# A bias that a rank-one matmul added, added by VectorE from a precomputed matrix

## The chip, the cores and the metric

The kernel runs on one core of a Trainium2 chip. The metric is the device time of the whole program in microseconds (us), lower is better. Engines are named as the profile names them: PE is TensorE's matmul, PEld its weight load, DVE is VectorE, ACT is ScalarE, POOL is GpSimd, SP is SyncE, which issues the DMAs.

## The reference, cut to what matters

The input is x of 8 batches x 1024 nodes x 128 features, and adj, a 1024 x 1024 matrix. Two blocks follow one another, each with a residual and a layer norm. The first is three graph layers whose weighting is adj squared element by element. The second is two graph layers with a bias, and then LSTMs over windows of 1, 2, 3 and 4 nodes; the last state of each window takes the place of its last node.

```python
h = relu(einsum('ts,bsh->bth', adj, x @ Wg0 + bg0))
h = relu(einsum('ts,bsh->bth', adj, h @ Wg1 + bg1))   # bg1 is the bias of this case
for p in range(1, 5):
    nw = T // p
    last = lstm_last(Wih[p-1], Whh[p-1], bih[p-1], bhh[p-1], h[:, :nw*p].reshape(B*nw, p, H))
    h = h.at[:, arange(nw)*p + (p-1)].set(last.reshape(B, nw, H))
```

Since adj @ (h @ Wg1 + bg1) = (adj @ h) @ Wg1 + rowsum(adj) x bg1, the bias of the second graph layer is an outer product: row sums of adj (one per node) times bg1 (one per feature). It is the same for every batch.

## The kernel before

**Numbers.** Every fp32 product is made of three matmuls on values that are split in a high and a low part (HI, LO): `product` at lines 514 to 518 issues them as L516, L517 and L518. So each result in PSUM is read twice: ACT writes HI with an activation (`hi_part`), then DVE writes LO as the difference (`lo_part` L966, or `lo_relu` L969 where a relu is in between).

**Stages.** The first block takes the batches in pairs (lines 530 to 647). The second block is a software pipeline of nine slots, 0 to 8. In slot n the graph layers of batch n are computed, and LSTM steps of the batches before it are put between them, so that PE has matmuls while ACT and DVE work. Slots 3 to 6 are a loop of two turns of two slots; the others are written out. The lists `SLOT`, `DRAIN` (slot 7) and `LAST` (slot 8), lines 256 to 279, set one order of items, and each engine goes through the same list in order, doing its own share of each item. No engine passes over an item that it waits for.

**Items that matter here.**
- `adj_x`, `wg0`, `adj_h`, `wg1` are the graph layers of a batch, each in two halves of 512 columns. `wg1` is the last: three matmuls of `product` on z (adj @ h) and the weights `wgs[:, i, 1, :]`, and then `bias_product`, L652, which adds brow x rowsum as one more matmul of 512 columns. ACT then writes h0 HI with a relu (L897, called at L950) and DVE h0 LO (L969, called at L1299).
- `wg0` has its bias already the other way: a matrix bias0 is made once in slot 0 (item `bias`, lines 762 to 768 and 936 to 939), DVE adds it to PSUM in place (L1288), ACT waits for that and writes HI (L943), DVE writes LO (L969).
- a step X, Y or Z with a window p and a step s is an LSTM step of a stream. PE makes its gates (3 for s = 0, else 4), ACT applies sigmoid or tanh to each (L911), DVE does the cell (L1208, or L1210, L1212, L1215), ACT the tanh (L921), DVE multiplies (L1229) and splits the state in HI and LO (L1246, L966) for the next step's matmuls. The tile is gates_x and hstep_x for X, gates and hstep for Y.
- `ahead` lets PE make the gates that don't depend on the state before it. The gates rotate through six PSUM banks: PE makes gate n only when ACT has acted on gate n - 6 (`gate_bank_free`, lines 696 to 700, checked before a step's first and third gate).
- `split` splits the next batch's x (ACT L818, DVE L966), `scale` is the layer norm's last part (L1024), `fin` puts the LSTM result back into xb (PE L805, DVE L1305).

**Order around the change** in slots 3 to 6: `adj_h` half 1, `split`, `wg1` half 0, step X 4 3, step Y 2 0, `wg1` half 1, `scale`, `fin` 0, step Y 2 1, `fin` 1. The cell of X 4 3 is finished together with Y 2 0. Slots 0 to 2 leave out what has no batch yet; in slot 1 the scaling of the last pair of the first block (`pair_scale`, L1024 x16) stands between Y 2 0 and `wg1` half 1. The first item of the next slot, Y 1 0, reads h0, so PE waits there for both halves.

Of the kernel before, what the change touches and what calls it, by code (L numbers as in the profile page):

```python
# [8 lines left out]
F32 = mybir.dt.float32  # L9
# [5 lines left out]
P = 128  # L15
# [24 lines left out]
def build(nc, x, adj_t, w1, w2, w3, wg0, bg0, wg1, bg1, wih_t, whh_t, bih, bhh, out):  # L40
# [10 lines left out]
    with ctx:  # L51
# [4 lines left out]
        def place(nbytes):  # L56
            at = top[0]
            top[0] += (nbytes + 63) // 64 * 64
            return at

        def sb(name, shape, dt, at=None):
            size = 4 * int(np.prod(shape[1:]))
            return nc.alloc_sbuf_tensor_at(name, shape, dt, offset=place(size) if at is None else at)
# [14 lines left out]
        adj_raw = sb("adj_raw", [P, MT, N], F32, big_at)  # L78
        lw = sb("lw", [P, 2, 2 * SKIPS - 1, G4], F32R, big_at)
        rowsum = sb("rowsum", [P, N], F32R, big_at + 28 * KB)  # L80
        r2_at = place(16 * KB)
        y2 = sb("y2", [P, 2, K2, N], F32R, r2_at)
        w0_raw = sb("w0_raw", [P, H1 + K2 * H2 + K3 * F], F32, r2_at)
# [66 lines left out]
        def sem(name):  # L150
            return ctx.enter_context(nc.semaphore(name))
# [21 lines left out]
        sum_mm, sum_hi, sum_lo = sem("sum_mm"), sem("sum_hi"), sem("sum_lo")  # L173
        bias_mm, bias_set = sem("bias_mm"), sem("bias_set")
        bias_add = sem("bias_add")
        lw_hi, lw_lo = sem("lw_hi"), sem("lw_lo")
        gate_mm = sem("gate_mm")
        gate_act = sem("gate_act")
# [334 lines left out]
        def _(pe):  # L513
# [136 lines left out]
            def bias_product(dst, stat, mov, start):  # L650

                return pe.matmul(dst, stat, mov, start=start, stop=True)  # L652

            def pe_slot(slot, turn):
# [18 lines left out]
                def mm_unit(r):  # L673
                    return ps[:, GB + r % 2, :]
# [8 lines left out]
                for item in items(slot):  # L683
# [43 lines left out]
                    elif item[0] == "adj_x":  # L727
                        _, half, m0, m1 = item
                        if m0 == 0:
                            bank_free(half)  # L730

                        def tile_split(m):
                            pe.wait_ge(b_lo, m + 1)
                        last = adj_by(mm_unit(half), lambda i, m: node[:, i, m * P:(m + 1) * P], half, m0, m1,
                                      tile_split if slot == 0 and half == 0 else None)
                        if m1 == MT:
                            last.then_inc(b_mm, 1)
                    elif item[0] == "wg0":

                        v = item[1]  # L740
                        bank_free(2 + v)
                        lo_reached(b_lo_of(slot, v))
                        for t in range(4):
                            nt = (4 * v + t) * P
                            dst = mm_unit(2 + v)[:, t * F:(t + 1) * F]
                            last = product(dst, lambda i: z[:, i, nt:nt + P], lambda i: wgs[:, i, 0, :],
                                           True, True)
                        last.then_inc(b_mm, 1)
                    elif item[0] == "rowsum":


                        pe.wait_ge(acc_lo, 1)
                        pe.wait_ge(const_set, 1)
                        for half in range(HALVES):
                            cols = slice(half * BANK, (half + 1) * BANK)
                            parts = [adj[:, i, m, cols] for m in range(ADDED, MT) for i in (HI, LO)]
                            parts += [h0[:, HI, cols], h0[:, LO, cols]]
                            for n, part in enumerate(parts):
                                last = pe.matmul(ps[:, half, :], ones[:], part, start=(n == 0),
                                                 stop=(n == len(parts) - 1))  # L760
                        last.then_inc(sum_mm, 1)
                    elif item[0] == "bias":

                        pe.wait_ge(sum_lo, 1)
                        for t in range(MT):
                            last = bias_product(ps[:, t // 4, t % 4 * F:(t % 4 + 1) * F],
                                                rowsum[:, t * P:(t + 1) * P], brow[:, 0, :], True)
                        last.then_inc(bias_mm, 1)
                    elif item[0] == "adj_h":
                        _, half, m0, m1 = item  # L770
                        if m0 == 0:
                            bank_free(4 + half)

                        def h_tile_ready(m):
                            lo_reached(b_lo_of(slot, 2 + m // 4))
                        last = adj_by(mm_unit(4 + half), lambda i, m: node[:, i, m * P:(m + 1) * P], half,
                                      m0, m1, h_tile_ready)
                        if m1 == MT:
                            last.then_inc(b_mm, 1)
                    elif item[0] == "wg1":  # L780

                        half = item[1]
                        bank_free(6 + half)
                        lo_reached(b_lo_of(slot, 4 + half))
                        cols = slice(half * BANK, (half + 1) * BANK)
                        product(mm_unit(half), lambda i: wgs[:, i, 1, :], lambda i: z[:, i, cols],
                                True, False)
                        bias_product(mm_unit(half), brow[:, 1, :], rowsum[:, cols], False).then_inc(b_mm, 1)
                    elif item[0] == "fin":

                        _, v, back = item
                        if v == 0:

                            last_step = before(slot, k, lambda w, b: b + w.back == back and w.p == SKIPS
                                               and w.s == SKIPS - 1)
                            pe.wait_ge(h_done, ahead("unit", slot, turn, k - last_step + 1))
                        if slot < B:
                            lo_reached(b_lo_of(slot, 6 + v))
                        else:

                            lo_reached(0)
                            pe.wait_ge(fin_add, ahead("fin", slot, turn, n_fin - 1))
                        for t in range(4):
                            at = (2 * v + t // 2) * OPEN_BLOCK + t % 2 * P
                            last = pe.transpose(mm_unit(v)[:, t * F:(t + 1) * F], full_in(slot, back)[:, at:at + P],  # L805
                                                ident_f[:])
                        last.then_inc(fin_mm, 1)
                        n_fin += 1
# [5 lines left out]
        def _(act):  # L814
# [78 lines left out]
            def act_slot(slot, turn):  # L893
                def hi_part(r, dst, func):

                    act.wait_ge(b_mm, ahead("mm", slot, turn, r + 1))
                    nc.scalar.activation(dst, ps[:, GB + r % 2, :], func).then_inc(b_hi, 1)  # L897

                k, gate, begun, n_ended = 0, 0, [], 0
                for item in items(slot):  # L900
# [29 lines left out]
                    if item[0] == "adj_x" and item[3] == MT:  # L930
                        hi_part(item[1], z[:, HI, cols], ACT.Copy)
                    elif item[0] == "rowsum":
                        act.wait_ge(sum_mm, 1)
                        nc.scalar.activation(h0[:, HI, :], ps[:, 0:2, :].rearrange("p a c -> p (a c)"),
                                             ACT.Copy).then_inc(sum_hi, 1)
                    elif item[0] == "bias":
                        act.wait_ge(bias_mm, 1)
                        for v in range(2):
                            nc.scalar.activation(bias0[v][:], ps[:, v, :], ACT.Copy).then_inc(bias_set, 1)
                    elif item[0] == "wg0":  # L940

                        act.wait_ge(bias_add, ahead("bias", slot, turn, item[1] + 1))
                        nc.scalar.activation(node[:, HI, cols], ps[:, GB + item[1], :], ACT.Relu).then_inc(b_hi, 1)  # L943
                    elif item[0] == "adj_h" and item[3] == MT:
                        hi_part(4 + item[1], z[:, HI, cols], ACT.Copy)
                    elif item[0] == "split":

                        x_hi(batch_of(slot, turn, -1), b_hi)
                    elif item[0] == "wg1":
                        hi_part(6 + item[1], h0[:, HI, cols], ACT.Relu)  # L950

            slots(act, act_slot)

# [8 lines left out]
        def _(dve):  # L962
# [220 lines left out]
            def dve_slot(slot, turn):  # L1183
# [12 lines left out]
                for item in items(slot):  # L1196
# [97 lines left out]
                    elif item[0] == "split":  # L1294
                        hi_ready(7)
                        x_lo(batch_of(slot, turn, -1), b_lo)
                    elif item[0] == "wg1":
                        hi_ready(7 + splits(slot) + item[1])
                        lo_relu(h0[:, LO, cols], ps[:, GB + item[1], :], h0[:, HI, cols], b_lo)  # L1299
                    elif item[0] == "fin":  # L1300
# [69 lines left out]
```

## Time and profile before

| | us |
|---|---|
| three runs, median (lowest to highest) | 1044.88 (1043.42 to 1046.79) |
| the profiled execution | 1043.99 |
| its span, first to last instruction | 1042.1 |
| TensorE's granted clock over the span, share of full speed | 0.991 |

The page gives each engine's busy time; the table of windows gives it for stretches of the span. The timeline has one line per instruction, or per run of equal ones: start, duration, engine, line, output and input, and in square brackets how long the engine had been idle and who released it. Durations of neighbours on one engine overlap, because they are pipelined, so what an instruction costs its engine is the distance from its start to the next start.

### The profile page before, as it was taken

What the parts mean: (1) busy time and instruction counts of PE and PEld (TensorE: products, weight loads), DVE (VectorE), ACT (ScalarE), POOL (GpSimd) and SP (SyncE); (2) the same over time, 40 slices, a digit from 0 to 9 for tenths busy, and PEclk for the clock granted to TensorE, in tenths of its full rate; (3) what the DMA queues carried; (4) which work ended last, traced back from release to release, by engine and by line L of the source; (5) the groups of instructions that cost most, each with busy time, mean ns of one, the idle gap of its engine ahead of it and who ended that gap; (6) DMA issues with size and microseconds to landing.
All of it is one profiled execution on the core that took longest, in us unless ns stands there. A gap on an engine that the chain in (4) does not pass through costs nothing.

```text
span 1042.1 us, 15018 instructions
## 1 busy us (share of the span) xinstructions
PE 1001.4 (96%) x5624; PEld 881.9 (85%) x5624; DVE 584.9 (56%) x1415; ACT 379.2 (36%) x696; POOL 19.8 (2%) x22
## 2 busy tenths in 40 slices
PE   5999999999999999999998999999999999999883
PEld 4888998889988899888987879898988989889782
DVE  7242533424334243342475576668677786777887
ACT  6221202212023120131334354546464454546652
POOL 0000000000000000000000000101010010100000
PEclk9999999999999999999999999999999999999997
DMA  9400000000000000000120000000000000000001
GB/s 315 124 1 1 1 1 1 1 1 2 1 0 0 0 0 0 0 0 0 56 105 1 1 1 1 1 1 1 21 1 21 0 20 0 21 1 21 1 15 46
DMA packets 21743, 20.42 MB, mean 20 GB/s; under 512 B 960, under 2 KB 18496, under 8 KB 21696
## 3 DMA queue, kind: packets, MB, share of 16 engines
q1 hardware_dynamic: 21696, 19.81, 6.0%
q8 instruction: 27, 0.44, 0.2%
q14 instruction: 20, 0.16, 0.1%
HBM read 15.61 MB, written 4.19 MB: 19 GB/s over the span
## 4 chain that ended last, share of the span: by engine, by line
PE 88%; DVE 8%; ACT 2%; issue 1%; DMA 0%; ACTq 0%; SPq 0%; DVEq 0%
PE ps L516 25%; PE ps L517 24%; PE ps L518 24%; PE ps L636 9%; PE ps L615 4%; PE ps L618 1%; DVE adj L966 1%; DVE xb L1024 1%; ACT gates_last L911 1%; PE ps L805 0%; DMA xb<-in_x 0%; DVE gates_last L1229 0%; DVE node L966 0%; PE ps L652 0%; DVE square L1032 0%
## 5 line engine op out<-in xcount | busy, mean ns | idle before, releaser
L516 PE MATMUL ps<-adj,node 128*128 128x512 f32 x384 | 151.6, 395 | 12.7 <-DVE adj L966 10.0
L517 PE MATMUL ps<-adj,node 128*128 128x512 f32 x384 | 150.5, 392 | 0.0
L518 PE MATMUL ps<-adj,node 128*128 128x512 f32 x384 | 150.4, 392 | 0.0
L966 DVE TENSOR_TENSOR y<-ps,y 128x512 fp32r<-128x512 f32 x48 | 33.1, 691 | 186.0 <-ACT y L851 186.0
L851 ACT ACTIVATE y<-ps 128x512 fp32r<-128x512 f32 x48 | 28.7, 598 | 294.5 <-PE ps L518 294.4
L516 PE MATMUL ps<-adj,h 128*128 128x512 f32 x256 | 99.7, 389 | 0.0
L517 PE MATMUL ps<-adj,h 128*128 128x512 f32 x256 | 99.7, 389 | 0.0
L518 PE MATMUL ps<-adj,h 128*128 128x512 f32 x256 | 99.6, 389 | 0.0
L516 PEld LDWEIGHTS ps<-adj,node 128*128 128x128 f32 x384 | 72.6, 189 | 28.0 <-DVE adj L966 10.7
L969 DVE SCALAR_TENSOR_TENSOR h<-ps,h 128x512 fp32r<-128x512 f32 x112 | 76.5, 689 | 35.2 <-ACT h L851 34.4
L636 PE MATMUL ps<-s,adj 128*128 128x256 f32 x768 | 93.0, 283 | 0.0
L636 PEld LDWEIGHTS ps<-s,adj 128*128 128x128 f32 x768 | 92.4, 192 | 0.0
L911 ACT ACTIVATE gates<-ps,lb 128x512 f32<-128x512 f32 (+2 forms) x117 | 70.7, 649 | 43.4 <-PE ps L518 29.3
L518 PEld LDWEIGHTS ps<-adj,node 128*128 128x128 f32 x384 | 72.5, 189 | 15.5
L517 PEld LDWEIGHTS ps<-adj,node 128*128 128x128 f32 x384 | 72.7, 189 | 14.0
L911 ACT ACTIVATE gates_x<-ps,lb 128x258 f32<-128x258 f32 (+1 forms) x156 | 67.2, 508 | 34.4 <-PE ps L518 34.4
L851 ACT ACTIVATE h<-ps 128x512 fp32r<-128x512 f32 x96 | 57.4, 597 | 48.9 <-PE ps L518 46.0
L615 PE MATMUL ps<-w3s,h 128*128 128x256 f32 x256 | 59.6, 333 | 0.0
L618 PE MATMUL ps<-w3s,h 128*128 128x128 f32 x256 | 56.9, 222 | 0.0
L518 PEld LDWEIGHTS ps<-adj,h 128*128 128x128 f32 x256 | 48.1, 188 | 10.1
L516 PEld LDWEIGHTS ps<-adj,h 128*128 128x128 f32 x256 | 48.1, 188 | 9.8
L517 PEld LDWEIGHTS ps<-adj,h 128*128 128x128 f32 x256 | 48.1, 188 | 9.7
(213 smaller groups left out, 2028.7 us busy)
## 6 DMA issues: line engine op xcount, KB each, us to landing
square<-in_adj_t SPq DMA_DIRECT2D x8, 512.0 KB, 8.1
xb<-in_x SPq DMA_DIRECT2D x8, 512.0 KB, 7.5
adj_raw<-in_adj_t SPq DMA_DIRECT2D x8, 512.0 KB, 8.4
out<-xb SPq DMA_DIRECT2D x7, 512.0 KB, 3.2
lw_raw<-in_wih_t SPq DMA_DIRECT2D x1, 1024.0 KB, 5.7
lw_raw<-in_whh_t SPq DMA_DIRECT2D x1, 768.0 KB, 7.2
w_raw<-in_w SPq DMA_DIRECT2D x1, 512.0 KB, 11.0
out<-xb SPq DMA_DIRECT2D x2, 256.0 KB, 2.5
```

The lines of the kernel that those rows point to most:

```text
L516: pe.matmul(dst, stat(HI), mov(HI), start=start, stop=False)
L517: pe.matmul(dst, stat(HI), mov(LO), start=False, stop=False)
L518: return pe.matmul(dst, stat(LO), mov(HI), start=False, stop=stop)
L615: pe.matmul(ps[:, q % BANKS, 2 * t * F:(2 * t + 2) * F], h2[:, HI, k, nt:nt + P], w3s[:, k, :, :].rearrange("p a c -> p (a c)"), start=(k ...
L618: last = pe.matmul(ps[:, q % BANKS, 2 * t * F:(2 * t + 1) * F], h2[:, LO, k, nt:nt + P], w3s[:, k, HI, :], start=False, stop=(k == K3 - 1) ...
L636: last = pe.matmul(dst, adj[:, a, m, nt:nt + P], s3[:, b, m, :, :].rearrange("p j c -> p (j c)"), start=(m == 0 and t == 0 and (a, b) == ( ...
L851: nc.scalar.activation(dst, ps[:, (j * A_MM + q) % BANKS, :], func).then_inc(a_hi, 1)
L911: nc.scalar.activation(gates_in(u.stream)[:, g, at], ps[:, (AHEAD["gate"][slot] + gate) % GB, 0:u.n], ACT.Tanh if g == GG else ACT.Sigmoid ...
L966: nc.vector.tensor_tensor(dst, src, f32(hi), ALU.subtract).then_inc(done, 1)
L969: nc.vector.scalar_tensor_tensor(out=dst, in0=src, scalar=0.0, in1=f32(hi), op0=ALU.max, op1=ALU.subtract).then_inc(done, 1)
L1024: last = nc.vector.tensor_scalar(rows, rows, mv[:, g, 0:1], newton[:, 1, g:g + 1], ALU.subtract, ALU.mult)
```

## The change

The bias of the second graph layer is computed once, in slot 0, as the matrix bias1 (128 features x 1024 nodes). Item `bias` gets two more matmuls of 512 columns on PE and two more copies on ACT; bias1 takes the place of rowsum, which nothing reads afterwards. In `wg1` the rank-one matmul is gone. DVE waits for the product (b_mm), adds bias1 to the PSUM bank in place and raises bias1_add; ACT waits for bias1_add where it waited for b_mm, and writes HI; DVE waits for ACT and writes LO as before. This stands in both halves of `wg1` in slots 0 to 7.

```diff
@@ sb tensors, semaphores
+        bias1 = sb("bias1", [P, N], F32, big_at + 28 * KB)
+        bias1_add = sem("bias1_add")
@@ pe_slot, item "bias"
                             last = bias_product(ps[:, t // 4, t % 4 * F:(t % 4 + 1) * F],
                                                 rowsum[:, t * P:(t + 1) * P], brow[:, 0, :], True)
+                        for half in range(HALVES):
+                            last = bias_product(ps[:, 2 + half, :], brow[:, 1, :],
+                                                rowsum[:, half * BANK:(half + 1) * BANK], True)
                         last.then_inc(bias_mm, 1)
@@ pe_slot, item "wg1"
                         product(mm_unit(half), lambda i: wgs[:, i, 1, :], lambda i: z[:, i, cols],
-                                True, False)
-                        bias_product(mm_unit(half), brow[:, 1, :], rowsum[:, cols], False).then_inc(b_mm, 1)
+                                True, True).then_inc(b_mm, 1)
@@ act_slot, item "bias"
+                        for v in range(2):
+                            nc.scalar.activation(bias1[:, v * BANK:(v + 1) * BANK], ps[:, 2 + v, :],
+                                                 ACT.Copy).then_inc(bias_set, 1)
@@ act_slot, item "wg1"
-                        hi_part(6 + item[1], h0[:, HI, cols], ACT.Relu)
+                        act.wait_ge(bias1_add, ahead("bias", slot, turn, item[1] + 1))
+                        nc.scalar.activation(h0[:, HI, cols], ps[:, GB + item[1], :], ACT.Relu).then_inc(b_hi, 1)
@@ dve_slot, item "wg1"
+                        if slot == 0:
+                            dve.wait_ge(bias_set, 4)
+                        dve.wait_ge(b_mm, ahead("mm", slot, turn, 6 + item[1] + 1))
+                        unit = ps[:, GB + item[1], :]
+                        nc.vector.tensor_tensor(unit, unit, bias1[:, cols], ALU.add).then_inc(bias1_add, 1)
                         hi_ready(7 + splits(slot) + item[1])
                         lo_relu(h0[:, LO, cols], ps[:, GB + item[1], :], h0[:, HI, cols], b_lo)
```

DVE's queue from `split` to `wg1` half 1 in slot 2, before (lines of the old file; [waits ...] names the semaphore):

```order
L966 TENSOR_TENSOR node<-xb,node 128x1024 [waits b_hi]
L969 SCALAR_TENSOR_TENSOR h_63<-ps,h_63 128x512 [waits b_hi]
L1210 TENSOR_TENSOR gates_x<-gates_x 128x258 [waits gate_act]
L1212 TENSOR_TENSOR gates_x<-gates_x 128x258 [waits gate_act]
L1215 TENSOR_TENSOR gates_x<-gates_x 128x258 [waits cell_step]
L1208 TENSOR_TENSOR gates<-gates 128x512 [waits gate_act]
L1224 TENSOR_TENSOR hfull<-gates_x 128x3x86 [waits tanh_done]
L1229 TENSOR_TENSOR gates<-gates 128x512 [waits tanh_done]
L1246 CAST hstep<-gates 128x512 [waits cell_step]
L966 TENSOR_TENSOR hstep<-gates,hstep 128x512 [waits cell_step]
L969 SCALAR_TENSOR_TENSOR h_63<-ps,h_63 128x512 [waits b_hi]
```

and after (lines of the new file, 8 higher on DVE):

```order
L974 TENSOR_TENSOR node<-xb,node 128x1024 [waits b_hi]
L1310 TENSOR_TENSOR ps<-ps,bias_59 128x512 [waits b_mm]
L977 SCALAR_TENSOR_TENSOR h_64<-ps,h_64 128x512 [waits b_hi]
L1218 TENSOR_TENSOR gates_x<-gates_x 128x258 [waits gate_act]
L1220 TENSOR_TENSOR gates_x<-gates_x 128x258 [waits gate_act]
L1223 TENSOR_TENSOR gates_x<-gates_x 128x258 [waits cell_step]
L1216 TENSOR_TENSOR gates<-gates 128x512 [waits gate_act]
L1232 TENSOR_TENSOR hfull<-gates_x 128x3x86 [waits tanh_done]
L1237 TENSOR_TENSOR gates<-gates 128x512 [waits tanh_done]
L1254 CAST hstep<-gates 128x512 [waits cell_step]
L974 TENSOR_TENSOR hstep<-gates,hstep 128x512 [waits cell_step]
L1310 TENSOR_TENSOR ps<-ps,bias_59 128x512 [waits b_mm]
```

An add (L1310) now stands ahead of each LO part of h0 (L977), and the LO part's wait for ACT is a wait for an activation that can only begin after that add.

ACT's queue over the same items of slot 2, before:

```order
L818 ACTIVATE node<-xb 128x1024
L897 ACTIVATE h_63<-ps 128x512 [waits b_mm]
L911 ACTIVATE gates_x<-ps,lb 128x258 [waits gate_mm,h_done]
L911 ACTIVATE gates_x<-ps,lb 128x258 [waits gate_mm] x3
L911 ACTIVATE gates<-ps,lb 128x512 [waits gate_mm,h_done]
L911 ACTIVATE gates<-ps,lb 128x512 [waits gate_mm] x2
L921 ACTIVATE gates_x<-gates_x 128x258 [waits cell_done]
```

and after:

```order
L822 ACTIVATE node<-xb 128x1024
L958 ACTIVATE h_64<-ps 128x512 [waits bias1_add]
L915 ACTIVATE gates_x<-ps,lb 128x258 [waits gate_mm,h_done]
L915 ACTIVATE gates_x<-ps,lb 128x258 [waits gate_mm] x3
L915 ACTIVATE gates<-ps,lb 128x512 [waits gate_mm,h_done]
L915 ACTIVATE gates<-ps,lb 128x512 [waits gate_mm] x2
L925 ACTIVATE gates_x<-gates_x 128x258 [waits cell_done]
```

No row moved on ACT; the activation of h0 waits for DVE where it waited for PE, and seven gate activations are queued behind it.

## Rows read from the trace of the kernel before

**Rows 1.** The page, busy time of PE and DVE over the span.

```profile
PE 1001.4 (96%) x5624; PEld 881.9 (85%) x5624; DVE 584.9 (56%) x1415; ACT 379.2 (36%) x696; POOL 19.8 (2%) x22
```

**Rows 2.** Table of windows, one loop slot: stretch, length, busy (instructions) per engine, clock, DMA.

```profile
788.00:846.00 58.00, 58.00 (x327) 51.52 (x326) 43.18 (x107) 30.02 (x59) 2.74 (x2) 1.00 0.03 10
```

**Rows 3.** Rank-one matmul: its group by shape, and the timeline around one.

```profile
L652 PE MATMUL ps<-rowsum,brow 128*128 128x512 f32 x16 | 6.3, 392 | 0.0
...
717.61 0.39 PE L652 MATMUL ps<-rowsum,brow 128*128 128x512 f32 x1
...
717.84 0.28 PE L516 MATMUL ps<-hw,lw 128*128 128x258 f32 x1
```

**Rows 4.** Timeline, item wg0 in a loop slot, ACT and DVE.

```profile
751.76 0.69 DVE L1288 TENSOR_TENSOR ps<-ps,bias_a 128x512 f32<-128x512 f32 x1
752.49 0.60 ACT L943 ACTIVATE node<-ps 128x512 fp32r<-128x512 f32 x1 [2.12 <-DVE ps L1288]
753.12 0.69 DVE L969 SCALAR_TENSOR_TENSOR node<-ps,node 128x512 fp32r<-128x512 f32 x1 [0.67 <-ACT node L943]
753.72 0.69 DVE L1288 TENSOR_TENSOR ps<-ps,bias_b 128x512 f32<-128x512 f32 x1
```

**Rows 5.** Timeline of slot 3 from wg1 half 0 to Y 2 1.

```profile
719.88 1.58 ACT L911 ACTIVATE gates_x<-ps,lb 128x258 f32<-128x258 f32 x4 [0.73 <-PE ps L518]
...
720.45 0.68 DVE L969 SCALAR_TENSOR_TENSOR h<-ps,h 128x512 fp32r<-128x512 f32 x1
...
721.05 0.52 DVE L1210 TENSOR_TENSOR gates_x<-gates_x 128x258 f32<-128x258 f32 x1
...
721.67 2.07 ACT L911 ACTIVATE gates<-ps,lb 128x512 f32<-128x512 f32 x3 [0.21 <-PE ps L518]
...
723.08 0.69 DVE L1208 TENSOR_TENSOR gates<-gates 128x512 f32<-128x512 f32 x1 [0.71 <-ACT gates L911]
...
725.78 0.69 DVE L966 TENSOR_TENSOR hstep<-gates,hstep 128x512 fp32r<-128x512 f32 x1
...
726.39 0.69 DVE L969 SCALAR_TENSOR_TENSOR h<-ps,h 128x512 fp32r<-128x512 f32 x1
...
726.89 0.48 PE L516 MATMUL ps<-hstep,lw 128*128 128x512 f32 x1
...
729.04 0.68 DVE L1305 TENSOR_TENSOR xb<-xb,ps 128x512 f32 x1
```

**Rows 6.** Timeline, end of slot 0: both LO parts of h0, then PE's Y 1 0.

```profile
571.50 1.28 DVE L969 SCALAR_TENSOR_TENSOR h<-ps,h 128x512 fp32r<-128x512 f32 x2
...
572.83 0.50 PE L516 MATMUL ps<-h,lw 128*128 128x512 f32 x1 [1.48 <-DVE h L969]
```

**Rows 7.** Timeline, end of slot 1, from wg1 half 0 to PE's Y 1 0.

```profile
604.64 1.85 ACT L911 ACTIVATE gates<-ps,lb 128x512 f32<-128x512 f32 x3
...
605.44 0.68 DVE L969 SCALAR_TENSOR_TENSOR h<-ps,h 128x512 fp32r<-128x512 f32 x1
...
613.33 0.68 DVE L969 SCALAR_TENSOR_TENSOR h<-ps,h 128x512 fp32r<-128x512 f32 x1
...
614.06 0.50 PE L516 MATMUL ps<-h,lw 128*128 128x512 f32 x1 [1.65 <-DVE h L969]
```

**Rows 8.** Timeline, end of slot 7: both halves of wg1, gates of Y 3 0 and X 4 1.

```profile
951.31 0.69 DVE L969 SCALAR_TENSOR_TENSOR h<-ps,h 128x512 fp32r<-128x512 f32 x1 [0.24 <-ACT h L897]
...
953.31 1.42 ACT L911 ACTIVATE gates<-ps,lb 128x344 f32<-128x344 f32 x3
...
954.10 0.68 DVE L969 SCALAR_TENSOR_TENSOR h<-ps,h 128x512 fp32r<-128x512 f32 x1
...
954.71 0.29 PE L516 MATMUL ps<-hw,lw 128*128 128x258 f32 x1
```

**Rows 9.** Table of windows, slot 8: PE idle, and the stretch after it.

```profile
984.10:987.10 3.00, 0.00 (x0) 0.00 (x0) 2.51 (x6) 1.15 (x3) 0.00 (x0) 0.95 0.00 0
986.90:990.30 3.40, 3.16 (x12) 3.10 (x13) 2.29 (x6) 1.27 (x3) 0.00 (x0) 0.51 0.00 0
```

## The prediction

> **What bounds the kernel now.** I read the page first: PE is busy 96% of the span, DVE 56% [rows 1]. That alone would say that a matmul saved is time saved, and that DVE has room. A share over the span hides who waits, so I then cut the span by slots. A loop slot takes 58.0 us, PE is busy in all of them and DVE in 43.2 [rows 2]. PE is the bound there, yet DVE has under 15 us to spare, and what counts is where. So the third view was the timeline around `wg1`, with one question per row: how long before PE needs this does DVE have it ready? In slot 3 the state of Y 2 0 (hstep, L966) is ready at 725.78 + 0.69 = 726.47, and PE takes it at 726.89 [rows 5]: 0.42 us of slack, directly behind `wg1` half 0 in DVE's queue. At the ends of slots 0 and 1 there is none: PE is already waiting for the LO part of h0 [rows 6, 7].
>
> **What is removed.** Sixteen rank-one matmuls, two in each of slots 0 to 7. Each lasts 0.392 us, but the next matmul starts 0.23 us after it [rows 3], and 0.23 is what it costs PE. Two of the same shape are added in slot 0. Net 14 x 0.23 = 3.2 us of PE, worth that only where PE does not wait. The bank, the weights and z are as before.
>
> **The price of the new step.** `wg0` shows the pattern: add at 751.76, ACT at 752.49 (+0.73), LO part at 753.12 (+0.63), next DVE instruction at 753.72 (+0.60) [rows 4]. So an item `wg1` holds DVE for 1.96 us where a LO part whose HI part was waiting held it for 0.60, as half 0 did from 720.45 to 721.05 [rows 5]: +1.36 us. I take these as the size, since shapes and engines are the same. The second effect is on ACT: its activation can't run until DVE has come to the add, and the gate activations are queued behind it.
>
> **A steady slot (2 to 6), half 0.** By the rows of slot 3 [rows 5]: the add starts at 720.45, where the LO part did; ACT's activation at 721.18; its gates of X 4 3 at 721.18 + 0.50 = 721.68 in place of 719.88 (four in 1.58); the gates of Y 2 0 behind them at about 723.17 in place of 721.67. DVE's L1208 was already waiting for these gates (0.71 idle before 723.08), so it moves by the same 1.50, and the chain behind it too. hstep is ready at 726.47 + 1.50 = 727.97, and PE starts on it at 728.02, not 726.89. PE's own work is two matmuls shorter, so it stands ready at 726.43 and idles 1.6 us. Net +1.13 a slot, the two saved matmuls included. The bound below, if only DVE's own 1.36 counts: 1.36 - 0.42 - 0.46 = +0.48. The bound above, if half 1 costs as much again: +1.13 + 1.36 = +2.5. I take 1.13, which follows ACT's queue. Five slots: **+5.7** (2.4 to 12.5).
>
> **Half 1 in these slots.** Its add takes the place of the LO part at 726.39 [rows 5], 1.50 later, at 727.89, and what follows on DVE is later by 1.50 + 1.36 = 2.9. The LO part ends at 727.89 + 1.36 + 0.69 = 729.94. PE then has Y 2 1's twelve matmuls (12 x 0.23 = 2.8 from 728.02), so `fin` 1 and the next slot's Y 1 0 find h0 ready. `scale`, the add of `fin` 0 (L1305) and Y 2 1's cell are queued behind it on DVE. L1305 moves from 729.04 [rows 5] to 731.9 and ends at 732.6. `adj_x` of the next slot needs it, after Y 2 1, four transposes (some 0.4) and the nine matmuls of Y 1 0: 728.02 + 2.8 + 0.4 + 2.1 = 733.3. Covered by 0.7 us; this is the thinnest cover that I rely on, and the rest of the slot (15 us idle, [rows 2]) takes the lag up.
>
> **Slot 0.** The two extra matmuls stand ahead of `wg0`, 2 x 0.23 = 0.46, and ACT's two extra copies end about as DVE's first add does: **+0.5**. At the end, both LO parts run in one go from 571.50 to 572.78 and PE starts at 572.83 [rows 6]. Now: add 571.50, activation 572.23, LO 572.86, add 573.46, activation 574.19, LO 574.82 to 575.51, PE at 575.56: **+2.7**. The matmuls removed there lie ahead of waits and save nothing.
>
> **Slot 1.** Half 0: the add at 605.44, activation at 606.17, Y 2 0's gates at 606.67 in place of 604.64 [rows 7], +2.03, of which 0.1 is absorbed, so what follows, with the scaling of the last pair, comes 1.96 later. Half 1's LO part began at 613.33; now the add begins at 615.29, the LO part 1.36 later at 616.65, PE at 617.38 in place of 614.06 [rows 7]: **+3.3**.
>
> **Slot 7.** No `split` here; DVE was idle 0.24 before the LO part at 951.31 [rows 8]. Half 0: the add can start when DVE is free, at 951.07 or, pipelined, 951.0; the LO part 1.36 later at 952.36, +1.05. Half 1: add at 954.10 + 1.05 = 955.15, activation 955.88, and behind it the gates of Y 3 0 at 956.38 in place of 953.31 [rows 8]. PE may make the third gate of X 4 1 only when the first of those has been read, at about 956.93. It made it at 954.71, or 954.25 with two matmuls less. So PE goes on at 956.98: **+2.3**. Slot 8 follows from there; its chain starts at those gates.
>
> **The clock.** PE stood still from 984.1 to 987.1, and the next 3.4 us ran at a granted clock of 0.51, the lower level of 1.2 GHz [rows 9]; that costs 3.4 x 0.49 = 1.7 us where PE is the bound. The end of slot 0 now has PE idle from about 571.4 to 575.6, 4.2 us, longer than that. I count one such stretch: **+1.7**. At the end of slot 1 PE would be idle 3.0 us, as long as the stretch of the rows; I leave it out of the sum and in the range.
> The Trainium skill ("TensorE: Matmul & The Clock Gate", Part 1: The HAM clock gate) says that the monitor runs free and does not start with the kernel, so a gap only some way longer than these may or may not be caught; by that, the slot 0 stretch is a toss-up and the time 1059.4 or 1061.1.
>
> **Sum.** 5.7 + 0.5 + 2.7 + 3.3 + 2.3 = 14.5; with the clock 16.2. The profiled execution is 1043.99 (span 1042.1), which gives 1060.2. It lies 0.9 below the median of the three runs, 1044.88, which gives 1061.1. I forecast **1061**.
>
> **Rivals.**
> - *DVE's room covers it.* PE waits only if hstep comes more than 0.42 + 0.46 = 0.88 us later in a steady slot. If the delay were under that point, at the ends of slots 0, 1 and 7 too, the time would be 1044.9 - 3.2 = 1041.7. For it: DVE 56% busy [rows 1]. Against: the add and the round trip alone are 1.36, and slots 0 and 1 have PE waiting today. A half-way form, delay under the point only at the steady slots, is 1044.9 + 8.8 - 5 x 0.46 = 1051.4.
> - *A cancelling mix.* The steady slots gain 0.46 each, and the ends cost little since DVE orders them better than my chain says: within 3 us of 1044.9. Nothing in the rows speaks for it.
> - *The thin cover breaks.* If `fin` 0's add comes late for `adj_x`, half 1's 1.36 reaches PE in slots 3 to 6: 4 x 1.36 = 5.4 more, 1066.5. It decides from 0.7 us of further delay on. For it: DVE's lag is 1.7 us against PE. Against: PE itself is later by then.
> - *The clock falls in slot 1 too, or in neither*: 1062.8 or 1059.4.
>
> **How the numbers follow.** A measurement of this kernel can tell a change of about 0.3%, 3.1 us, from none. Forecast with either clock (1055 to 1065): 0.70. Thin cover, or more of its kind (above 1065): 0.12. Half-way form (1048 to 1055): 0.11. Cancelling mix: 0.04. Covered, 1041.7: 0.03. The low end takes in the half-way form, the high end the broken cover with a second slow stretch (1066.5 + 1.7): 1051 to 1068. Slower 0.93, same 0.04, faster 0.03.
>
> **What the profile after would show.** L652 at 512 columns only twice. Sixteen adds of 0.69, and behind each an activation of h0 that DVE released. The idle time of PE: some 4 us at the end of slot 0, 3 at the end of slot 1, 1.3 to 1.6 before each hstep of Y 2 1 released by DVE hstep, some 2.7 in X 4 1 of slot 7 released by ACT. Slots 3 to 6 at 59.1 in place of 58.0. Wrong it would be if PE still had no gap in the loop slots, or if a gap stood before `adj_x`, or if the clock stayed at 1.00 up to slot 8.

## The result, and the profile after

| | before | after |
|---|---|---|
| median of four runs (lowest to highest), us | 1045.2 (1043.42 to 1046.79) | 1063.74 (1061.63 to 1066.78) |
| the profiled execution, us | 1043.99 | 1063.89 |
| its span, us | 1042.1 | 1062.2 |
| granted clock over the span | 0.991 | 0.985 |

The change makes the kernel slower: the ratio is 1.0183 (95% interval 1.0166 to 1.0200), which is +19.1 us on 1044.9; the two medians themselves are 18.5 apart. The forecast was 1061.0, range 1051 to 1068.

The page after, PE and DVE [rows 1]:

```profile
PE 1006.0 (95%) x5610; PEld 882.1 (83%) x5610; DVE 596.5 (56%) x1431; ACT 378.1 (36%) x698; POOL 19.6 (2%) x22
```

PE has 14 matmuls fewer and is nevertheless busy 4.6 us longer. In part this is the clock: the first matmul of a stretch lasts 0.80 at the lower clock and 0.50 at the full one (576.19 below, and rows 6). In part it is how busy time is counted: a matmul that the next one follows at once adds 0.23, one in front of a gap its whole 0.39. DVE's busy time rises by 11.6 us, and its share stays at 56%. The shares show none of the 19 us.

The view that shows it is PE's table of waits (what was waited for: us in total, times, longest). After:

```profile
PE ps L518 <- DVE hstep L974: 8.2, 8, 2.2
PE ps L518 <- DVE h L977: 5.9, 2, 4.4
...
PE ps L518 <- ACT gates L915: 2.5, 1, 2.5
...
PE ps L518 <- DVE hstep_x L974: 1.5, 1, 1.5
...
PE ps L518 <- DVE xb L1318: 1.2, 1, 1.2
```

In before the same table has 2.3 us (2 times) for hstep and 3.1 (2 times) for h, and nothing for the other three. So by these five rows PE waits 13.9 us more: in nine new places, and longer at the end of slot 0.

Next, the timeline at three of them. End of slot 0 after, where rows 6 showed one pair of LO parts:

```profile
572.13 0.69 DVE L1310 TENSOR_TENSOR ps<-ps,bias 128x512 f32<-128x512 f32 x1
572.85 0.60 ACT L958 ACTIVATE h<-ps 128x512 fp32r<-128x512 f32 x1 [1.90 <-DVE ps L1310]
573.48 0.69 DVE L977 SCALAR_TENSOR_TENSOR h<-ps,h 128x512 fp32r<-128x512 f32 x1 [0.66 <-ACT h L958]
574.09 0.69 DVE L1310 TENSOR_TENSOR ps<-ps,bias 128x512 f32<-128x512 f32 x1
574.81 0.60 ACT L958 ACTIVATE h<-ps 128x512 fp32r<-128x512 f32 x1 [1.36 <-DVE ps L1310]
575.44 0.69 DVE L977 SCALAR_TENSOR_TENSOR h<-ps,h 128x512 fp32r<-128x512 f32 x1 [0.66 <-ACT h L958]
...
576.19 0.80 PE L518 MATMUL ps<-h,lw 128*128 128x512 f32 x1 [4.43 <-DVE h L977]
```

Two round trips DVE, ACT, DVE in a row; DVE stands still 0.66 in each. Slot 3 after (compare rows 5):

```profile
729.67 0.69 DVE L1310 TENSOR_TENSOR ps<-ps,bias 128x512 f32<-128x512 f32 x1
730.39 0.60 ACT L958 ACTIVATE h<-ps 128x512 fp32r<-128x512 f32 x1 [2.50 <-DVE ps L1310]
730.89 1.57 ACT L915 ACTIVATE gates_x<-ps,lb 128x258 f32<-128x258 f32 x4
...
732.32 1.87 ACT L915 ACTIVATE gates<-ps,lb 128x512 f32<-128x512 f32 x3
...
733.64 0.69 DVE L1216 TENSOR_TENSOR gates<-gates 128x512 f32<-128x512 f32 x1 [0.63 <-ACT gates L915]
...
736.24 0.69 DVE L974 TENSOR_TENSOR hstep<-gates,hstep 128x512 fp32r<-128x512 f32 x1
...
736.98 0.50 PE L518 MATMUL ps<-hstep,lw 128*128 128x512 f32 x1 [0.72 <-DVE hstep L974]
```

ACT sits idle for 2.50 us until DVE has added, with seven gates behind. Slot 7 after (compare rows 8; the first line is the slot's start):

```profile
920.12 0.47 PE L518 MATMUL ps<-adj,node 128*128 128x512 f32 x1 [1.21 <-DVE xb L1318]
...
971.10 0.69 DVE L1310 TENSOR_TENSOR ps<-ps,bias 128x512 f32<-128x512 f32 x1
...
971.83 0.60 ACT L958 ACTIVATE h<-ps 128x512 fp32r<-128x512 f32 x1 [1.89 <-DVE ps L1310]
...
972.91 0.58 PE L518 MATMUL ps<-hw,lw 128*128 128x258 f32 x1 [2.53 <-ACT gates L915]
```

To sum it up I set each matmul of after beside the same one of before and read how much later it starts. This shift (in us, as all that follow) is 0.16 at the start of slot 0, and then grows: bias matrix +0.48, end of slot 0 +2.72, clock behind it +1.65, slot 1 +3.31, five steady slots +4.49 (0.87 to 0.96 each), a wait for hstep_x at the start of slot 5 +1.67, a wait at the start of slot 7 +1.47, the end of slot 7 +2.25, slots 7 and 8 +1.84 (a slow stretch behind slot 7's wait +2.86, one of before's missing -1.40, a wait for hstep_last +0.38). Together 20.04, against a span that is 20.1 longer.

### The profile page after: what moved, and what is told of

The parts are those of the page before. It is cut to its first block, busy times and chain, and to the rows that moved or that the text cites. A ratio compares the mean times of both kernels' runs of the same rounds, so it can differ in the third digit from the quotient of the medians.

```text
span 1062.2 us, 15010 instructions
## 1 busy us (share of the span) xinstructions
PE 1006.0 (95%) x5610; PEld 882.1 (83%) x5610; DVE 596.5 (56%) x1431; ACT 378.1 (36%) x698; POOL 19.6 (2%) x22
## 4 chain that ended last, share of the span: by engine, by line
PE 80%; DVE 12%; ACT 5%; issue 2%; DMA 0%; DVEq 0%; ACTq 0%; SPq 0%
PE ps L518 22%; PE ps L519 22%; PE ps L520 22%; PE ps L638 8%; PE ps L617 4%; PE ps L620 1%; ACT gates_x L915 1%; DVE xb L1032 1%; ACT gates L915 1%; DVE node L974 1%; DVE ps L1310 1%; DVE gates L1237 1%; DVE adj L974 1%; ACT gates_last L915 1%; DMA xb<-in_x 0%
## 5 line engine op out<-in xcount | busy, mean ns | idle before, releaser
L518 PE MATMUL ps<-adj,node 128*128 128x512 f32 x384 | 151.5, 395 | 14.5 <-DVE adj L974 10.6
L977 DVE SCALAR_TENSOR_TENSOR h<-ps,h 128x512 fp32r<-128x512 f32 x112 | 76.8, 691 | 45.6 <-ACT h L855 34.3
L519 PEld LDWEIGHTS ps<-adj,node 128*128 128x128 f32 x384 | 72.6, 189 | 13.9
L915 ACT ACTIVATE gates<-ps,lb 128x512 f32<-128x512 f32 (+2 forms) x117 | 69.0, 652 | 28.1 <-PE ps L520 13.9
```

What stands on the lines that cost most here:

```text
L518: pe.matmul(dst, stat(HI), mov(HI), start=start, stop=False)
L519: pe.matmul(dst, stat(HI), mov(LO), start=False, stop=False)
L915: nc.scalar.activation(gates_in(u.stream)[:, g, at], ps[:, (AHEAD["gate"][slot] + gate) % GB, 0:u.n], ACT.Tanh if g == GG else ACT.Sigmoid ...
L977: nc.vector.scalar_tensor_tensor(out=dst, in0=src, scalar=0.0, in1=f32(hi), op0=ALU.max, op1=ALU.subtract).then_inc(done, 1)
```

## The experiments

My theory: the time comes from the round trip (ACT waits for DVE, DVE for ACT), which holds up both queues. The main rival: it is DVE's extra work. nobias, trip, work, half0 and half1 are the kernel before with one edit; early0, early01, warm, swap, unroll and mix are the kernel after with one edit. Ratios are to the kernel before on the same chip, with 95% intervals, and a time difference given beside one is that ratio applied to before's 1044 to 1045 us; the medians themselves can differ from it by up to 1.3 us (work: 7.6 in place of 6.3). Line numbers differ by a few between kernels. "By the shift" means measured as above, matmul by matmul against before's trace.

The runs that test the theory cost more than I expected of them, by 2 to 6 us each (trip, work, half0, half1, early0, early01). In their traces much of that is slow stretches of the clock, which I had not counted.

**nobias: the second layer's bias left out altogether.** This bounds what removing the rank-one matmuls can bring.

```diff
@@ pe_slot, item "wg1"
-                                True, False)
-                        bias_product(mm_unit(half), brow[:, 1, :], rowsum[:, cols], False).then_inc(b_mm, 1)
+                                True, True).then_inc(b_mm, 1)
```

> The kernel before without the sixteen rank-one matmuls, and nothing in their place: the second graph layer's bias is left out of what is computed. It prices what the change removes. If a removed matmul is worth its distance to the next one, 0.23 us, wherever PE doesn't wait (slots 1 to 7, two each): 14 x 0.23 = 3.2 us less than before, about 1042. If it hides behind something, no difference.

Measured: 1042.53, ratio 0.9980 (0.9971 to 0.9989), -2.1 us. In its trace slots 2 to 7 are each 0.46 shorter, as two matmuls are, 2.8 us in all. In slot 1 nothing is left of it: PE comes earlier to hstep and waits 0.49. The profiled execution also has a slow stretch at the end of slot 0 that before's has not. So some 0.2% (0.1 to 0.3 by the interval) was to be had here.

**trip: the round trip without the work.** The rank-one matmul is kept. Where the change has DVE's add there is a memset of one column (0.06 us), and ACT waits for it.

```diff
@@ act_slot, item "wg1"
-                        hi_part(6 + item[1], h0[:, HI, cols], ACT.Relu)
+                        act.wait_ge(bias1_add, ahead("bias", slot, turn, item[1] + 1))
+                        nc.scalar.activation(h0[:, HI, cols], ps[:, GB + item[1], :], ACT.Relu).then_inc(b_hi, 1)
@@ dve_slot, item "wg1"
+                        dve.wait_ge(b_mm, ahead("mm", slot, turn, 6 + item[1] + 1))
+                        nc.vector.memset(took_wait[:, 0:1], 0.0).then_inc(bias1_add, 1)
```

> The kernel before, rank-one matmuls kept, but ACT's activation of h0 waits for a tiny DVE instruction (a memset of one column, 0.06 us) that stands where the add stands in the changed kernel. It has the round trip DVE to ACT to DVE and no work. If the coupling of the two queues is the cause: +1.5 at the end of slot 0, +2.1 in slot 1, +0.5 in each of slots 2 to 6, +1.0 in slot 7, in all about +7 (1052). If DVE's added work is the cause: within 1 us of before.

**work: the work without the round trip.** The rank-one matmul is kept, ACT waits for PE as before, and DVE does one more 128x512 operation on a matrix that it leaves as it is.

```diff
@@ dve_slot, item "wg1"
+                        nc.vector.tensor_tensor(bias0[item[1]][:], bias0[item[1]][:], bias0[item[1]][:], ALU.max)
```

> The kernel before, rank-one matmuls kept, with one more DVE instruction of the add's shape (128x512, 0.69 us, on SBUF, without effect on any value) ahead of each LO part of h0; ACT waits for PE as before. It has the work and no round trip. If the coupling is the cause, this costs only where PE already waits for DVE: 2 x 0.60 at the end of slot 0 and 2 x 0.60 in slot 1, and nothing in slots 2 to 6 where DVE's L1208 waits 0.71 us for ACT anyway: about +2.4 (1047.5). If DVE's work is the cause: +10 or more.

Measured: trip 1056.04, 1.0116 (1.0101 to 1.0132), +12.1; work 1051.64, 1.0060 (1.0045 to 1.0076), +6.3. The order is as the theory has it, but neither size is: both cost about 4 to 5 more than I expected. PE's waits in trip, then in work:

```profile
PE ps L517 <- DVE h L971: 5.5, 2, 3.0
...
PE ps L517 <- DVE hstep_x L968: 1.0, 1, 1.0
PE ps L517 <- ACT gates L912: 0.9, 1, 0.9
PE ps L517 <- DVE xb L1309: 0.6, 1, 0.6
```

```profile
PE ps L516 <- DVE h L969: 4.9, 2, 2.7
PE ps L516 <- DVE hstep L966: 2.9, 3, 1.2
...
PE ps L516 <- DVE xb L1306: 0.4, 1, 0.4
```

In work no steady slot is longer; the wait for h at the ends of slots 0 and 1 grows, since two more DVE operations lie straight on PE's way there. The wait for xb at the start of slot 7 adds 0.6 by the shift. The rest is the clock: the table of windows of work has these three slow stretches and a fourth one around 596, where before's trace has none.

```profile
558.10:561.50 3.40, 3.40 (x11) 2.71 (x10) 2.78 (x5) 3.40 (x7) 0.00 (x0) 0.61 0.02 5
575.40:579.60 4.20, 4.14 (x10) 3.27 (x11) 4.16 (x35) 1.38 (x2) 0.00 (x0) 0.50 0.00 0
622.20:625.80 3.60, 3.56 (x9) 2.84 (x10) 2.83 (x5) 0.63 (x1) 0.00 (x0) 0.53 0.01 2
```

By the shifts the three cost 1.5, 2.7 and 1.5 us, and the fourth 1.6. This profiled execution, 1054.32, is the slowest of work's four, so the median holds less of them; how much less isn't shown. So the rival explains about a third (4.7 to 7.9 us of 19.1 by the interval), and nothing in a steady slot. In trip the surplus is a wait for hstep_x in slot 5 (1.2 by the shift), the wait for xb (0.9) and one slow stretch (1.4). Both kernels have the wait for xb that I had thought covered.

In a steady slot trip costs 0.3, work nothing, and the change 0.9, though it has two matmuls less. The parts don't add up, and the trace of trip says why. Its memset begins at 726.19, and ACT follows 0.11 later, where it follows the start of an add by 0.72:

```profile
726.30 0.60 ACT L952 ACTIVATE h<-ps 128x512 fp32r<-128x512 f32 x1 [1.92 <-DVE took_wait L1301]
```

ACT's gates are late by 0.61 more with an add than with a memset, and that is the difference between 0.3 and 0.9. So the add's length does count, but only because ACT waits for it inside the round trip.

**half0 and half1: the change in one half of `wg1` only**, the other half as before.

```diff
@@ dve_slot, item "wg1" (cut; PE's and ACT's shares have the same condition)
+                        if item[1] == 0:    # half1: item[1] == 1
+                            ...
+                            nc.vector.tensor_tensor(unit, unit, bias1[:], ALU.add).then_inc(bias1_add, 1)
```

> The change in half 0 of wg1 only; half 1 keeps its rank-one matmul. If the cost comes from ACT's and DVE's queues as worked out: +0.2 for the matrix, +1.4 at the end of slot 0, +2.0 in slot 1, +1.1 in each of slots 2 to 6 (one matmul saved in place of two), +0.3 in slot 7: about +9.5 against before (1054.5). PE's gap before hstep of Y 2 1 is there in every loop slot, none before adj_x in slot 7.

> The change in half 1 of wg1 only; half 0 keeps its rank-one matmul. As worked out: +0.2 for the matrix, +1.4 at the end of slot 0, +1.4 in slot 1, a saved matmul (-0.23) and no gap before hstep in slots 2 to 6, +1.2 in slot 7, and +1 to +2 where DVE's lag reaches PE (X 3 1 of slot 5, adj_x of slot 7): about +4.5 against before (1049.7). If half 1 costs in the steady slots as half 0 does: +10.

Measured: half0 1057.28, 1.0111 (1.0089 to 1.0134), +11.6; half1 1052.26, 1.0078 (1.0057 to 1.0099), +8.1. Waits of half0, then of half1:

```profile
PE ps L519 <- DVE hstep L983: 6.9, 8, 2.1
PE ps L519 <- DVE h L986: 2.8, 1, 2.8
PE ps L519 <- ACT gates L921: 0.3, 1, 0.3
```

```profile
PE ps L519 <- DVE h L986: 6.1, 2, 3.1
...
PE ps L519 <- ACT gates L921: 1.3, 1, 1.3
PE ps L519 <- DVE xb L1328: 1.1, 1, 1.1
PE ps L519 <- DVE hstep_x L983: 0.4, 1, 0.4
```

This parts the terms. The steady slots are half 0's alone: 0.9 each in half0's trace by the shift, and in half1's none is longer. The wait for xb at the start of slot 7 is half 1's alone. The wait for hstep_x is none with half 0 alone, 0.4 with half 1 alone and 1.5 together; in early0 below, where half 0's add stands earlier, it is still 1.4.

**early0 and early01: the same adds, earlier in DVE's queue.** In early0 the add of half 0 stands ahead of `split`'s LO part, so that ACT's activation runs while DVE splits. In early01 the add of half 1 is also moved ahead, behind the cell before it (in slot 0, both adds ahead of both LO parts).

```diff
@@ dve_slot; add_bias(half) holds the wait for b_mm and the add
 elif item[0] == "split":
+    add_bias(0)
     hi_ready(7)
     x_lo(batch_of(slot, turn, -1), b_lo)
@@ early01 besides: in the step before ("wg1", 1), behind its cell
+    if adds_next:
+        add_bias(1)
```

> The changed kernel, with DVE's add of half 0 moved one item ahead, before the LO part of the next x (item split), while DVE waits for ACT anyway. Same instructions, other order. If the round trip is the cost, ACT's activation is no longer behind DVE's 1.4 us for x, and the gaps before hstep in slots 2 to 6 go: the saved matmuls count, -0.46 a slot. Left are slot 0 (+1.6), slot 1 (+1.2), slot 7 (+2.3 and the clock behind it), and DVE's lag from half 1 (+1 to +3): about +7 against before (1052). If the add's own time is the cost: 1063 as the changed kernel.

> As the one before, and the add of half 1 too is moved ahead, to directly behind the first cell product of the LSTM step before it (Y 2 0, in slot 7 X 4 0); in slot 0 both adds stand ahead of both LO parts. Same instructions. If the waits are the cost: slot 0 +1.5, slot 1 +0.5, slots 2 to 6 -2.3 together, slot 7 +0.7: about +1 against before (1046). If the adds' own time is the cost: 1063.

Measured: early0 1056.46, 1.0121 (1.0097 to 1.0144), +12.6; early01 1047.74, 1.0029 (1.0018 to 1.0041), +3.0. In early01 the adds and the dependencies are those of the change, DVE is about as busy (593.7 us, against 596.5), and 16 of the 19 us are gone. In early0's timeline DVE goes from `split` through the LO part to hstep without a wait for ACT's h0, in slot 3:

```profile
727.54 1.65 DVE L974 TENSOR_TENSOR node<-xb,node 128x1024 fp32r<-128x1024 f32 x1
729.12 0.68 DVE L977 SCALAR_TENSOR_TENSOR h<-ps,h 128x512 fp32r<-128x512 f32 x1
```

Its steady slots are 0.45 shorter than before's, the two matmuls. What is left in early0 is half 1: the waits for h, hstep_x (1.4), xb (1.1) and gates (2.5). It came out 5.6 above what I expected; two slow stretches behind the ends of slots 0 and 1 are 2.2 and 1.6 of it by the shifts, and the waits of slot 1 another 1.1. In early01 xb is gone, hstep_x is 0.3 and gates 0.8. So the loss hangs on where the add stands, and DVE's 0.69 us costs little by itself. This is the strongest evidence against the rival.

**warm: 16 matmuls that nothing reads, at the end of slot 0,** in the gap of 4.4 us.

```diff
+if slot == 1:
+    for _ in range(16):
+        pe.matmul(ps[:, 5, :], wgs[:, HI, 1, :], z[:, HI, 0:BANK], start=True, stop=True)
```

> The changed kernel with sixteen matmuls of 512 columns (16 x 0.23 = 3.6 us) into an unused PSUM bank, put where PE idles 4.4 us at the end of slot 0. Nothing reads them. If the idle stretch is what brings the clock down to 0.50 behind it: the clock stays at 1.00 there and the time is 1.7 us less than the changed kernel's, about 1062. If the clock has another cause: the same as the changed kernel or longer.

Measured: 1061.04, 1.0160 (1.0144 to 1.0176), 2.7 below the median of the kernel after; the intervals of the two ratios overlap at their ends. Its window behind the gap stays at full clock, where after's has half:

```profile
576.00:580.00 4.00, 4.00 (x18) 3.27 (x19) 3.96 (x31) 2.55 (x4) 0.00 (x0) 1.00 0.00 0
```

```profile
576.10:579.70 3.60, 3.51 (x8) 2.84 (x9) 3.56 (x25) 1.84 (x3) 0.00 (x0) 0.50 0.00 0
```

The first is warm's, the second after's. That the clock stayed up there in this execution, with matmuls in the gap, is shown, and the 1.65 us of that term with it (1.63 by the shift of warm against after). The median can't be put down to it, though. In slot 7, where nothing was changed, PE has the same wait in both traces (2.54 and 2.53, for ACT's gates), and in warm full clock follows it, in after half:

```profile
974.00:977.50 3.50, 3.50 (x20) 3.21 (x19) 3.33 (x11) 2.83 (x6) 0.00 (x0) 1.00 0.00 0
```

That is worth another 2.7 us between the two traces; whether it is chance or comes of the edit, no run shows.

**swap: `fin` 0 ahead of `scale`** in the loop slots, for the wait for xb in slot 7; **unroll: the loop of slots 3 to 6 written out**, for the wait for hstep_x at the loop's turn.

```diff
@@ swap, SLOT (lines joined)
-    ("wg1", 1), ("scale", 3), ("ahead",), ("fin", 0, 2), step(Y, 2, 1)
+    ("wg1", 1), ("ahead",), ("fin", 0, 2), ("scale", 3), step(Y, 2, 1)
@@ unroll, slots()
-    with eng.Fori(0, TURNS) as turn: ...
+    for slot in range(SLOTS):
+        body(slot, None)
```

> The changed kernel with the items scale and fin 0 exchanged in the loop's list, so that DVE adds fin 0 (L1318) before it scales (2.1 us) and not after. If the 1.2 us that PE idles before adj_x at the start of slot 7 is DVE's lag behind the half 1 add, that idle time goes: -1.5 against the changed kernel (about 1062). The wait in X 3 1 of slot 5 stays, since scaling is still ahead of Y 2 1's cell. If that idle time has another cause: no difference.

> The changed kernel with slots 3 to 6 written out in place of the loop of two turns; the instructions of each slot and their order are the same. In the changed kernel's trace DVE begins slot 5 2.8 us after its last instruction with nothing to wait for (issue), and in X 3 1 PE then waits 1.5 us. If the loop's turn is the cause: this wait goes, -1.7 against the changed kernel (about 1062), with slots 3, 4, 5 and 6 alike. If DVE's lag alone is the cause: the wait stays, or is in every slot.

Measured: swap 1063.61, 1.0186 (1.0170 to 1.0202); unroll 1063.37, 1.0182 (1.0167 to 1.0198). Neither moved the time, both traces moved the wait. In swap it stands five microseconds further on, for hw, and is hardly shorter (1.21 before the edit):

```profile
924.98 0.43 PE L518 MATMUL ps<-hw,lw 128*128 128x344 f32 x1 [1.06 <-DVE hw L974]
```

DVE is late as a whole there, and an item put forward makes the next one late. In unroll the wait for hstep_x is gone, and the shift does not grow between slots 4 and 6 but for the 0.9 of a steady slot. In the looped kernel DVE stood 2.77 us at the turn with nothing in the profile to wait for, written out 0.74 for ACT (the looped kernel, then unroll):

```profile
808.55 0.69 DVE L1216 TENSOR_TENSOR gates<-gates 128x512 f32<-128x512 f32 x1 [2.77 <-issue]
```

```profile
807.37 0.69 DVE L1211 TENSOR_TENSOR gates<-gates 128x512 f32<-128x512 f32 x1 [0.74 <-ACT gates L910]
```

unroll's profiled execution is 1.4 below after's, as the lost wait is worth, but the medians differ by 0.4, and each ratio has 1.6 us either way. So the cause of that wait is shown, its worth in the median is not.

**mix: what the others suggest, put together.** Rank-one matmuls in slots 0 and 1, where PE waits anyway; from slot 2 on the matrix, with both adds early; `fin` 0 ahead of `scale`.

```diff
@@ pe_slot, item "wg1" (cut; ACT and DVE have the same condition)
+if slot >= 2:
     product(..., True, True).then_inc(b_mm, 1)
+else:
+    product(..., True, False)
+    bias_product(mm_unit(half), brow[:, 1, :], rowsum[:, cols], False).then_inc(b_mm, 1)
```

> Rank-one matmuls in slots 0 and 1, where PE waits for DVE; in slots 2 to 7 the add, each moved ahead as in early01; scale and fin 0 exchanged. bias1 is kept in hfull until slot 2, where one ACT copy brings it to its place. If the removed matmul is worth 0.23 us where DVE has the time, and the waits are the only cost: +0.5 for the matrix, 0 in slots 0 and 1, -2.3 in slots 2 to 6, +0.7 in slot 7, 0 to +0.6 in X 3 1: -1 against before (1044), no more than -2. If the adds cost by themselves: +3 or more.

Measured: 1044.05, 0.9991 (0.9982 to 1.0000), against 1044.93. In its trace slots 2 to 7 gain 0.2 to 0.4 each (nobias: 0.46), and a wait of 0.83 at the end of slot 7 takes some back:

```profile
957.51 0.39 PE L518 MATMUL ps<-hw,lw 128*128 128x258 f32 x1 [0.83 <-ACT gates L924]
```

Here the add is hidden almost in full. But what it frees is so little that the result can't be told from the kernel before.

## Why the prediction was right, and where it was not

**Direction and mechanism: right, and shown.** trip, half0, half1, early0 and early01 leave the round trip in two strict queues as the cause. *DVE's room covers it* fell with the waits that follow each add; the work alone costs nothing in a steady slot, so the room was there, and the order of the queues kept the kernel from using it. The bound that counted only DVE's own 1.36 (+0.48 a slot) was too low, and so was the one that let half 1 cost as much again too high: half 0 alone makes the 0.9.

**Steady slots: 5.7 predicted, 4.5 in the trace.** The chain held link by link. Moved by the shift of 9.22 at that slot, the prediction put the add at 729.67, ACT at 730.40, the gates of X 4 3 at 730.90, those of Y 2 0 at 732.39, L1216 at 733.80 and PE at 737.24; the trace has 729.67, 730.39, 730.89, 732.32, 733.64 and 736.98. The 0.26 too much is the chain behind ACT: I kept the 2.07 us of the three gates from a trace in which ACT waited for PE between them. With PE ahead they took 1.87, and the steps behind them were 0.1 shorter.

**PE idle before hstep: 1.6 predicted, 0.72 seen.** Part of the same loss stood elsewhere: the third gate of Y 2 0 needs a bank that ACT's late gates had not given back, and PE lost some 0.36 there first. The rows of the matmuls have no wait in brackets; that of the weight load names ACT:

```profile
730.93 0.40 PE L520 MATMUL ps<-ht,lw 128*128 128x512 f32 x1
731.41 0.19 PEld L518 LDWEIGHTS ps<-ht,lw 128*128 128x128 f32 x1 [0.52 <-ACT gates_x L915]
731.41 0.50 PE L518 MATMUL ps<-ht,lw 128*128 128x512 f32 x1
731.75 0.40 PE L519 MATMUL ps<-ht,lw 128*128 128x512 f32 x1
```

The starts are 0.48 and 0.34 apart, where 0.23 is the rule. The view counts idle time only from a matmul's end, which lies after the start of the next in a full queue, so a wait is better read from start to start.

**Slots 0 and 1: right.** Bias matrix 0.5 predicted, 0.48 measured; end of slot 0 2.7 and 2.72; slot 1 3.3 and 3.31; the LO part of half 1 there, moved by the shift of 4.99, stood at 621.64 in the prediction and begins at 621.63. PE was waiting already, so that each link reached it undamped, and all links had durations in the trace of before. Only the place of the gap in slot 1 was wrong: not 3 us at its end, but 2.22 before hstep of Y 2 0, from half 0's delay, and 1.45 at the end, where it had been 1.65.

**End of slot 7: 2.3 predicted, 2.25 measured,** by the mechanism named: the third gate of X 4 1 waits 2.53 for ACT (2.7 by the shift, less the two matmuls).

**The thin cover: a wrong step.** I let the add of `fin` 0 be covered before `adj_x` by 0.7 us, with 2.1 us of Y 1 0's matmuls among the cover. That is true of slots 3 to 6, and no gap stands there. Slot 7 uses the list DRAIN, in which `adj_x` comes first and Y 1 0 behind it. Without the 2.1 the cover is -1.4, and 1.21 us of idle was seen, 1.47 by the shift. My own sign of being wrong, a gap before `adj_x`, came up in the one slot whose list I had not read.

**Slot 5: a term that was missing, +1.67.** I costed X 4 3 and the Y steps and said that 15 us of idle time would take up the lag. The idle time was there in the sum, but not where the lag met the loop's turn. In before DVE stands 1.93 us at the turn into slot 5, where it stands 0.82 at the same place of slots 4 and 6:

```profile
795.04 0.69 DVE L1208 TENSOR_TENSOR gates<-gates 128x512 f32<-128x512 f32 x1 [1.93 <-ACT gates L911]
```

In after it stands 2.77, against 0.81 in slot 4. So to DVE's lag of about 3 us the turn adds 2.0 in place of 1.1, and PE waits 1.47 for hstep_x. The window of [rows 2] covers just this slot, but as a sum it could not show it.

**The clock: one stretch predicted at +1.7; it was +1.65 at that place and 1.46 more at the end.** Another slow stretch in slot 1 lay beside a wait that set the end anyway. Behind the gap of slot 7 the clock fell again (+2.86), which I had not counted, and one of before's slow stretches in slot 8 was missing (-1.40):

```profile
975.30:978.80 3.50, 3.50 (x14) 3.13 (x14) 1.97 (x5) 2.96 (x7) 0.00 (x0) 0.50 0.00 0
```

So of 20.0 us 13.2 were the terms of the sum without the clock (14.5 predicted), 3.1 two waits that I missed, 3.1 the clock (1.7 predicted), and 0.5 rests. Against the profiled execution the sum was 3.7 too low, against the median 2.7. It was no more because the 1.2 too much in the steady slots paid for part of what was missing. That is luck, and so is part of the clock: warm's trace has the same gap in slot 7 and no slow stretch behind it, 2.7 us less.

## What to carry to other kernels

Before moving work from the busiest engine to one with room, write out both queues behind the new wait: the price is the round trip, the operation's length included, plus what stands behind it in each queue, not the busy time that it adds. Put the new operation in the queue ahead of some other work of that engine, so that its answer comes back meanwhile; here that alone was worth 16 us of 19. And where a schedule has several lists or a loop's turn, go through a cover in each of them.

## What the hardware showed that I had not expected

**The clock fell after short waits.** In work a wait of 0.88 us was followed by the slow stretch at 558 shown above:

```profile
557.50 0.80 PE L516 MATMUL ps<-adj,node 128*128 128x512 f32 x1 [0.88 <-DVE node L969]
```

In before's trace the same wait of 0.88 at this place, ended 0.09 later, is followed by full clock:

```profile
557.00:561.00 4.00, 3.41 (x15) 2.86 (x16) 3.33 (x6) 2.82 (x6) 0.00 (x0) 1.00 0.01 4
```

In nobias the stretch behind the end of slot 0 ran at 0.54, after waits of 0.71 and 1.71, where before's, after 0.48 and 1.48, ran at 1.00. By the shifts a stretch cost 1.4 to 2.9 us where no wait hid it. In the prediction I had gone by one row alone, with a gap of 3 us. The Trainium skill ("TensorE: Matmul & The Clock Gate", Part 1) says that the monitor is free-running and that its effect varies from run to run; the traces agree in that the same place, behind the same wait, had either level in two kernels. One kernel varies as well: six of early01's ten executions took 1046.4 to 1048.0 us at a mean granted clock of 0.987 to 0.989, the other four 1049.3 to 1049.7 at 0.985. What else sets it, these runs don't tell. It moves single executions by one to three us, which is about as much as the whole saving at stake.

**A loop's turn held DVE for 1 to 2 us.** DVE stood 2.77 us in the looped kernel where it stood 0.74 with the loop written out. In before it was 1.93 against 0.82 in the slots without a turn, unseen because DVE had slack. Why it was 1.1 there and 2.0 in the kernel after, no run shows.
